# A graph layer's segment sum: a counting sort with plain indirect moves in place of accumulating ones

## The reference

```python
ones = jnp.ones_like(src, dtype=jnp.int32)
in_deg = jnp.minimum(jax.ops.segment_sum(ones, dst, num_segments=num_nodes), MAX_IN_DEGREE - 1)
out_deg = jnp.minimum(jax.ops.segment_sum(ones, src, num_segments=num_nodes), MAX_OUT_DEGREE - 1)
edge_proj = edge_attr @ W_sum + b_sum
sum3d = jax.ops.segment_sum(edge_proj, src, num_segments=num_nodes)
cent_term = jax.nn.sigmoid(centralities @ W_cent + b_cent)
vor_term = jax.nn.sigmoid(voronoi_values @ W_vor + b_vor)
return x + z_in[in_deg] + z_out[out_deg] + cent_term + vor_term + sum3d
...
h = jnp.maximum(_layernorm(x, axis=-1), 0.0)
x = x + _L0_gnn_ref(h, edge_index, edge_attr_128, node_vec1, node_vec1_n2, ...)
```

## Time and profile before

| | |
|---|---|
| median of 3 runs | 3316.97 us (3316.22 to 3322.48) |
| span of the profiled execution | 3322.0 us |
| POOL busy | 2656.5 us (80%) |
| PE busy | 2369.6 us (71%), mean granted clock 0.729 |
| DVE busy | 1614.5 us (49%) |
| ACT busy | 837.3 us (25%) |
| transfers | 289.37 MB, 87 GB/s on the mean |

### The profile page before, as it was taken

One profiled execution on the slowest core, in us unless ns is written; L12 is line 12 of the kernel. 1 busy time (PEld: TensorE's weight loads), 2 busy tenths in 40 slices (PEclk: granted clock), 3 DMA queues, 4 the chain that ended last, 5 costly groups with the idle time before them and its releaser, 6 DMA issues.

```text
span 3322.0 us, 47400 instructions
## 1 busy us (share of the span) xinstructions
PE 2369.6 (71%) x16487; PEld 2137.9 (64%) x16487; DVE 1614.5 (49%) x4701; ACT 837.3 (25%) x2796; POOL 2656.5 (80%) x1681
## 2 busy tenths in 40 slices
PE   5788888888888888888765656565656665656539
PEld 4677777777777777777655656565656555656537
DVE  6444444444555555555544444444444444444416
ACT  1222222222222222222233222223232323232212
POOL 3788888888888888888888888888888888888850
PEclk7566666666766666666688777878787788788869
DMA  9555555555545454445454454544545445454469
GB/s 324 97 82 91 82 83 98 82 87 86 83 68 73 67 75 67 67 68 73 66 75 67 67 75 67 75 67 67 75 68 75 67 67 75 68 75 67 51 110 308
DMA packets 317909, 289.37 MB, mean 87 GB/s; under 512 B 32456, under 2 KB 285276, under 8 KB 317674
## 3 DMA queue, kind: packets, MB, share of 16 engines
q0 software_dynamic: 239184, 108.96, 36.1%
q1 hardware_dynamic: 75658, 164.58, 16.0%
q10 hardware_dynamic: 2832, 12.80, 1.0%
HBM read 144.90 MB, written 141.32 MB: 86 GB/s over the span
## 4 chain that ended last, share of the span: by engine, by line
POOL 66%; issue 17%; DMA 10%; PE 4%; DVE 1%; ACT 1%; POOLq 0%; ACTq 0%; SPq 0%; DVEq 0%
POOL table L361 66%; DMA table<-summed,index_area 10%; PE bank L793 2%; PE bank L801 1%; ACT summed L662 1%; PE bank L741 1%; PE bank L728 0%; DMA index_area<-in_src_dram 0%; PE bank L725 0%; DMA index_area<-table 0%; DVE base L415 0%; DVE base L416 0%; DVE base L412 0%; PE bank L701 0%; PE bank L762 0%
## 5 line engine op out<-in xcount | busy, mean ns | idle before, releaser
L361 POOL DMA_INDIRECT table<-summed,index_area x1661 | 2651.2, 1596 | 555.6 <-issue 467.3
L728 PE MATMUL bank<-edge_ring,same 128*128 128x128 f32 x3320 | 880.4, 386 | 828.0 <-ACT summed L662 671.9
L728 PEld LDWEIGHTS bank<-edge_ring,same 128*128 128x128 f32 x3320 | 718.1, 283 | 887.7 <-issue 480.3
L662 ACT ACTIVATE summed<-bank 128x512 f32<-128x512 f32 x416 | 248.1, 596 | 2338.9 <-DMA table<-summed,index_area 2333.4
L741 PE MATMUL bank<-hot_lo,hot_hi 128*128 128x100 bf16 x3322 | 651.0, 365 | 0.0
L458 DVE TENSOR_TENSOR seen<-bank,look_bits 128x16 f32<-128x16 f32 x416 | 72.5, 174 | 969.8 <-PE bank L732 969.7
L741 PEld LDWEIGHTS bank<-hot_lo,hot_hi 128*128 128x128 bf16 x3322 | 467.3, 147 | 106.5
L725 PE MATMUL bank<-edge_ring,cross 128*128 128x128 f32 x1660 | 459.8, 374 | 0.0
L441 DVE TENSOR_TENSOR same<-bank,index_area 128x512 f32<-128x512 f32 x416 | 283.5, 681 | 321.0 <-PE bank L701 320.9
L483 DVE TENSOR_TENSOR hot_hi<-index_area,iota_hi 128x1024 bf16<-128x1024 bf16 x416 | 288.8, 694 | 302.6 <-PE bank L741 288.8
L725 PEld LDWEIGHTS bank<-edge_ring,cross 128*128 128x128 f32 x1660 | 387.4, 287 | 0.0
(11 more groups left out here) (80 smaller groups left out, 1249.9 us busy)
## 6 DMA issues: line engine op xcount, KB each, us to landing
edge_ring<-in_edge_attr_dram SPq DMA_DIRECT2D x166, 640.0 KB, 4.1
table<-summed,index_area POOLq DMA_INDIRECT x1661, 3.4
table<-z_parts SPq DMA_DIRECT2D x48, 400.0 KB, 3.6
base<-in_x_dram SPq DMA_DIRECT2D x20, 560.0 KB
out_dram<-base ACTq DMA_DIRECT2D x16, 672.0 KB
index_area<-table SPq DMA_DIRECT2D x24, 384.0 KB, 7.4
edge_ring<-table SPq DMA_DIRECT2D x24, 384.0 KB, 7.2
base<-in_x_dram SPq DMA_DIRECT2D x20, 65.0 KB
```

What stands on the lines that cost most here:

```text
L361: g.indirect_dma_start(tables[t][:, :], bass.IndirectOffsetOnAxis(src_i[:, c:c + 1], 0), summed[:, q % SUM_SLOTS, i * F:(i + 1) * F], None ...
L662: a.activation(summed[:, q % SUM_SLOTS, 0:n * F], ps_sum[q % 2][:, 0:n * F], ACT.Copy).then_inc(s_evac, 1)
L728: t_.matmul(ps_sum[q % 2][:, t * F:(t + 1) * F], same[:, q % 2, t * P:(t + 1) * P], row, start=not second, stop=True)
```

## The change

The rows of the edges are no longer added in DRAM. They are sorted by window of nodes with plain indirect moves, read back in sorted order, and summed by products with one-hot matrices.

The edges are cut in four segments of 25, 175, 130 and 86 quads. For each segment:

- `totals` builds for each quad a one-hot of its 512 edges over the 100 windows (window = `src` % 100), and TensorE adds them up over the segment and all partitions in `ps_total`.
- `starts` turns these counts into the first row of each (window, tile of the quad) in the sorted area of the segment; `make_lists` (item `lists`) makes from it the list of pieces of 256 sorted rows: where each begins and which window it belongs to.
- For each quad, `rank` adds to the running starts in PSUM (`ps_rank`) a product that gives each edge its place and marks it by 2^18, ACT reads it with four accumulating relu (`positions`), DVE turns it to integers (`index`), `rebase` takes the mark away and moves the starts on, and GpSimd moves the four tiles' rows from the edge ring straight to the sorted area. A row is now 130 floats: 128 features, a 1 that counts, and a key that ACT writes (`row_keys`).
- When all moves of a segment have landed, its pieces are read back (SP, `Rows.load`, 128 partitions x 2 rows x 520 bytes, with the row number from a register), each gets a one-hot over 125 nodes (DVE, `piece`), two f32 products sum it (PE), and DVE adds it to the piece before if both are of one window (`fold`). ACT stores the running sums, two pieces at a time, to `sums` in DRAM.

The pieces of segments 0 to 2 (150, 450 and 360) are done beside the moves of the segments after them; a planner with a budget of 5.1 us per quad for DVE, PE and ACT places them, with `hist` (now for `dst` only), `stats` and `node`. The 270 pieces of segment 3 come after the last move. With a lag behind the last 100 of them run, window by window: the loading of the four segments' sums, their turning and adding (four products), the out-degree (from the counted column), the bias, the product with `W_sum`, and two additions of z rows. The z rows are fetched by 200 plain indirect gathers of 125 rows on GpSimd. All stores of the output are issued by SP after its last load.

What goes: the tables and their zeroing, `spread`, `quad`, `combine`, `rows`, `cast`, `match`, the out-degree part of `hist`, `z_split`, `spread_degrees`, `pick_z`.

```diff
 P = 128
-TABLES = 3
-PAIR = 2
 QUAD = 4
-LOAD_TILES = 10
-EDGE_SLOTS = 4
+LOAD_TILES = 5
+EDGE_SLOTS = 6
...
+SEGMENT_QUADS = (25, 175, 130, 86)
+ROW_GROUPS = (2, 2, 2, 2)
...
+BUDGET = 5.1
+BACKLOG = 2.0
+
+BASE = (0.55, 1.2, 2.5)
+COST = {"keys": (8.0, 0.0, 0.0), "totals": (0.36, 0.4, 0.0), "starts": (2.0, 0.0, 0.0), "lists": (8.0, 2.0, 0.0),
+        "hist": (0.8, 0.8, 0.0), "stats": (0.62, 0.0, 0.0), "degrees": (2.0, 0.0, 0.0), "indegrees": (0.3, 0.0, 0.0),
+        "early": (0.0, 0.0, 1.0), "node": (2.3, 0.0, 1.3), "piece2": (0.83, 0.75, 0.3)}
...
@@ SP: reading pieces back
+                row = self.values[c % ROWS_LOADED]
+                eng.dma_start(piece_ring[:, n % PIECE_SLOTS, 0:ROW_GROUPS[s], :].rearrange("p k f -> p (k f)"),
+                              area[s][bass.ds(row, rows_in[s]), :].rearrange("(p k) f -> p (k f)", k=ROW_GROUPS[s])
+                              ).then_inc(s_piece_in[n % PIECE_SLOTS], 16)
@@ SP: loads of edges, and the stores at the end
+                sp.dma_start(edge_ring[:, g % EDGE_SLOTS, :, 0:F],
+                             edge[0:FULL * P, :].rearrange("(p t) f -> p t f", p=P)[
+                                 :, g * LOAD_TILES:(g + 1) * LOAD_TILES, :]).then_inc(s_edge[g % EDGE_SLOTS], 16)
...
+            for w0, w1 in zip(store_start, store_start[1:]):
+                sp.wait_ge(s_added, w1)
+                for p0, p1 in ((0, WIDE_P), (WIDE_P, NODE_P)):
+                    sp.dma_start(by_partition(out)[p0:p1, w0:w1, :], base[p0:p1, w0:w1, :]).then_inc(s_out, 16)
@@ GpSimd: the moves
             for q in range(NQ):
-                pool.wait_ge(s_rows, q + 1)
-                pool.wait_ge(s_evac, q + 1)
...
-                    g.indirect_dma_start(tables[t][:, :], bass.IndirectOffsetOnAxis(src_i[:, c:c + 1], 0),
-                                         summed[:, q % SUM_SLOTS, i * F:(i + 1) * F], None,
-                                         compute_op=ALU.add).then_inc(s_scatter[t], 16)
+                pool.wait_ge(s_index, q + 1)
+                for t in tiles(q):
...
+                        if at == 0:
+                            pool.wait_ge(s_row_key, load + 1)
+                        g.indirect_dma_start(rows, bass.IndirectOffsetOnAxis(index, 0), edge_ring[:, slot, at, :],
+                                             None).then_inc(s_scatter[slot], 16)
@@ DVE: a piece, and its fold
+                v.scalar_tensor_tensor(out=hot_n[:, n % HOT_SLOTS, 0:G, :],
+                                       in0=iota_ps.unsqueeze(1).to_broadcast([P, G, LOC]),
+                                       scalar=wkey[:, s % 2, c:c + 1],
+                                       in1=piece_ring[:, n % PIECE_SLOTS, 0:G, KEY:ROW].to_broadcast([P, G, LOC]),
+                                       op0=ALU.add, op1=ALU.is_equal).then_inc(s_hot_n, 1)
...
+                    v.scalar_tensor_tensor(out=to, in0=stage[0:LOC, (n - 1) // STAGE % STAGES, (n - 1) % STAGE, :],
+                                           scalar=same[0:LOC, s % 2, c:c + 1], in1=new,
+                                           op0=ALU.mult, op1=ALU.add).then_inc(s_staged, 1)
@@ DVE: the main loop, with the last segment behind it
+            for q in range(NQ):
+                if q + 1 < NQ:
+                    hot_rows(q + 1)
+                for what, s, i in side[q] + (after if q == NQ - 1 else []):
...
+                index(q)
+            ahead = pieces[NS - 1] - SW
+            dve.wait_ge(s_node, NW)
+            for c in range(pieces[NS - 1] + ADD_LAG):
+                if c < pieces[NS - 1]:
+                    piece(NS - 1, c)
+                for at, k, w in z_order:
+                    if at == c and k == 0:
+                        add_z(k, w)
+                if ahead + COUNT_LAG <= c < pieces[NS - 1] + COUNT_LAG:
+                    count_out(c - ahead - COUNT_LAG)
+                if c >= ahead + ADD_LAG:
+                    add_product(c - ahead - ADD_LAG)
@@ ACT: an edge's place
+                for t in range(QUAD):
+                    last = a.activation(junk[:, t, :], part[:, t // 2, :, t % 2], ACT.Relu, bias=mark_col[:, :],
+                                        accum_out=pos_f[:, q % 4, t:t + 1])
+                last.then_inc(s_pos, 1)
@@ PE: an edge's place, and a piece
+                t_.matmul(ps_rank, before_b[:, :], hot, start=False, stop=True,
+                          skip_group_check=True).then_inc(s_rank, 1)
...
+                t_.matmul(ps_rank, after_b[:, :], hot, start=False, stop=False, skip_group_check=True)
+                t_.matmul(ps_rank, unmark_b[:, :], hot, start=False, stop=True, skip_group_check=True).then_inc(s_based, 1)
...
+                for k in range(ROW_GROUPS[s]):
+                    last = t_.matmul(to, hot_n[:, n % HOT_SLOTS, k, :], piece_ring[:, n % PIECE_SLOTS, k, 0:SUM], start=(k == 0),
+                                     stop=(k == ROW_GROUPS[s] - 1))
```

1230 lines of the change are left out of this document (712 added, 518 removed).

## The result

The changed kernel takes **3182.05 us** (median of 3 runs, 3174.68 to 3188.57) against 3316.97 before: a ratio of **0.959, 95% interval 0.957 to 0.962**. The direction was right, the size was not: 432 us over the forecast of 2750, and outside the range that ended at 3100.

A forecast was written before the change was run, and what follows sets the result against it. POOL, preparing one 128-row move every 1.85 us, was taken as the bound. Head 42, moves 2159, transfer stretch 50 and tail 505 gave 2756, said as 2750 us; forecast 2640 to 2870 (55%), range 2560 to 3100.

The forecast's parts named there:

- The price of a move: Plain indirect move on POOL: 1.00 us busy, 1.30 us in all, 2159 us for 1661 moves.
- Rival A: Plain moves cost POOL the same as accumulating ones: 3620 us, slower; 13%.
- C: Plain moves cheaper still, 0.8 us busy, so DVE, PE and transfers decide in segments 2 and 3: 2530 us; 12%.
- DVE against POOL: During moves, DVE at 85% could hold POOL up 0.09 us a move, 150 us; the skill's rule says nothing added.
- The head: Before the first move, with zeroing gone: first move near 37 us, put at 42 us.
- Beside the moves: Work during segment 3's moves, per four moves: DVE 4.2 us, PE 4.4, ACT's readings 1.84, all under POOL's 5.2.
- Transfers: Segment 3: 5.4 us per four moves at 290 GB/s against POOL's 5.2; 50 us allowed, bounds 0 and 570.
- The tail: After the last move, 270 pieces of the last segment and the windows, DVE last: 505 us, bounds 440 and 700.
- The sign that the prediction named for a wrong tail: After the last move, DVE's one-hot waits for SP or a transfer in most of its idle time.
- the far bound: After the last move, up to 700 us: SP at 1.28 us an issue, 474 us by itself, or PE at half clock.
- Rival B: Beside the moves something else bounds: scattered writes, SP's issues, PE at half clock, or DVE-PE waits; 3040 to 3320 us; 20%.
- Its other sign: Beside the moves: transfers over 95%, along with POOL idle before its moves that grows from segment 1 to 3.

The follow-up runs named there:

- the old kernel by itself: The kernel before with its moves no longer accumulating, nothing else changed: 3026.08 us on chip 4, a single run (before beside it 3314.81).
- the fastest version: Changed kernel with sums over 128 partitions, direct loads of early sums, 576-byte rows, segments of 50, 170, 115, 81 quads, LOAD_LAG 12: 2811.05 us, ratio 0.847.
- the one edit: Changed kernel with sums stored, copied and loaded over 128 partitions instead of 125: 2868.56 us, ratio 0.864, on chip 13 (control 3176.99).

## Why the prediction was right or wrong

**The price of a move: right.** 1.00 busy and 1.30 in all were forecast, 1.011 and 1.32 came, in the change and (0.983) in the old kernel by itself. The reading of the accumulating move as three accesses and the plain one as two gave a good number; it is not thereby shown to be the reason. The reasoning behind the number stays untested, so part of the hit may be luck. In packets the difference is larger than in POOL's time: the software queue went from 239184 packets at 36.1% to 78752 at 13.8%.

**Rival A fell, and C.** Both hung on the price, which the one number settled: 958 ns in the middle, not 1546 and not 800.

**DVE against POOL: not tested at the forecast's load.** The mean of a move stood 50 ns over its middle before and stands 53 over it now, with DVE at 60% of the span instead of 49%. But the worry was DVE at 85%, and it never got there. The nearest is segment 2 of the fastest version, with DVE at 76%; the mean move of that kernel is 1009 ns with 958 in the middle, 51 over. The Trainium skill's rule that the prediction drew on (SBUF — State Buffer, "Who interferes with whom"), that this kind of DVE work locks less, is not contradicted.

**The head: right** within 8 us, 34 for 42.

**Beside the moves: two terms a bit small.** A one-hot takes 0.473 us (0.42 to 0.48 was forecast), a fold 0.343 (0.29), so a piece is 0.82 instead of 0.76 on DVE; ACT's four readings are 4 x (0.340 + 0.202) = 2.17 us instead of 1.84. Neither decides: DVE is busy 131 of 250 us in segment 3.

**Transfers: this is the step that failed, twice over.** The paragraph summed bytes, divided by one rate of 290 GB/s, and allowed 50 us, "bounds: 0" and 570. The bytes fit what came: dividing them by the rate that was measured once all 16 engines worked, 252 GB/s, gives 1.35 MB / 252 = 5.4 us for four moves in segment 2 and 1.58 / 252 = 6.3 in segment 3, that is 1.34 and 1.57 a move; 1.37 and 1.58 came. So the rate was too high even for evenly spread transfers, and over 128 partitions the moves took 2292 us instead of 2209: 83 us over, on top of the 50 allowed. The larger part, 161 us beside the moves, I did not see at all: a rate belongs to a transfer of a certain shape, and stores over 125 partitions don't have it. The same code splits `x` and the output into 112 and 13 partitions, which I had in front of me and took for a detail. It was the trace of before itself that misled: its large transfers went evenly, and its row of 298 GB/s stood for "transfers" in general. The upper bound of 570 came from a wrong mechanism, the 80 ns of an accumulating packet. In the packet records of after a plain move is 16 packets of 8 rows each (4160 bytes), 195 ns on the mean, 24 a row. The bound was also added up wrongly, with 73 and 117 sets of four moves where the segments have 86 and 130; with these it is 652.

**The tail: the same step.** 505 was forecast with DVE last, 440 to 700 as bounds; 685 came, and 552 with the one edit. The sign that the prediction named for a wrong tail is there (waits of DVE between 2487 and 3172 us):

```profile
DVE hot_n L645 <- DMA piece_ring<-sorted: 176.8, 56, 13.0
```

Of DVE's 296 idle us, 177 are its one-hot waiting for a piece's transfer. DVE is busy 389 us of it where 425 and 32 of handovers were forecast, so DVE's work was put rather too high and the waits too low. SP's issues were the right suspect for the far bound, but not at 1.28 us each: nearly all take 0.27 to 0.33, and a few, behind the large loads, 4 to 7. PE was expected at the full clock because it would be pressed; it was busy for 417 of 685 us, at a granted clock of 0.74 (0.86 over 128 partitions). "DVE over 85% busy" in the tail was wrong with 389 of 685 (57%).

**Rival B was what happened**, inside the 3040 to 3320 that it was given at 20%, with the place that was named for it: nothing in segment 1, and idle of POOL released by `pos_i` after it. Its other sign did not show: transfers were to be over 95%, and the mean stood at 84%. A reader who went by that sign would have ruled B out; only the five engines were full. Of its four mechanisms it was transfers, though not for scattered writes. It was told as a mere sum of mishaps, "half of the bounds above", and that is why it carried only 20%. Had its mechanism been looked for (which transfers have a number of partitions that 16 doesn't divide), it could have been the forecast.

**The account of the 417 us** by span: -8 head, +244 moves, +180 tail. By the edit 161 of the 244 and 133 of the 180 go, and 2 us of head come back: 292 together (the two profiled spans; the medians on chip 13 say 308). What stays, 83 and 47, I put down to the lower rate of the full engines and the handovers of the tail; this split is argued.

## What to carry to other kernels

Before adding up the bytes of new transfers, look at the partition count of each: here a store over 125 partitions ran on 5 engines, one over 128 on 16, and three rows of padding were worth 308 us. A share of the transfer engines that hardly moved under different loads while GB/s stayed low was, here, full engines beside emptier ones; the small packets per issue told on how many a transfer ran. A wait that goes without the time going with it (ACT's "issue", 633 to 204 us for 55 us) is a sign of the limit, not the limit. When an engine that had covered everything gets faster, put the next limit into the forecast as the main case with a mechanism of its own, and compare variants only where the control ran on the same chip.
